# A decoder of four layers on one core: six layer normalisations moved to the head of the stages that follow them

## The reference

```python
def _layernorm(x, axis=-1, eps=1e-05):
    m = jnp.mean(x, axis=axis, keepdims=True)
    v = jnp.var(x, axis=axis, keepdims=True)
    return (x - m) / jnp.sqrt(v + eps)

x = x + attn(_layernorm(x), ...)          # L0 capped, L1 token mixing, L2 and L3 grouped-query
x = x + cross(_layernorm(x), ctx, ...)    # L3: the WKV recurrence with keys _layernorm(x), values ctx
x = x + ffn(_layernorm(x), ...)           # L0 MLP, L1 experts, L2 16 experts (4 chosen) + a shared one, L3 ternary
```

## Time and profile before

| | before |
|---|---|
| median of 3 runs | 1465.18 us (1462.57 to 1465.30) |
| the profiled execution's own time | 1461.6 us |
| its span, first to last instruction | 1459.9 us |
| mean granted TensorE clock | 0.893 of full speed |
| TensorE matmuls busy | 1221.0 us, 84% |
| TensorE weight loads busy | 755.3 us, 52% |
| VectorE busy | 794.9 us, 54% |
| ScalarE busy | 510.2 us, 35% |
| GpSimd busy | 319.6 us, 22% |
| mean DMA rate | 33 GB/s |

### The profile page before, as it was taken

One profiled execution on the slowest core, in us unless ns is written; L12 is line 12 of the kernel. 1 busy time (PEld: TensorE's weight loads), 2 busy tenths in 40 slices (PEclk: granted clock), 3 DMA queues, 4 the chain that ended last, 5 costly groups with the idle time before them and its releaser, 6 DMA issues. The chain is left out here.

```text
span 1459.9 us, 22518 instructions
## 1 busy us (share of the span) xinstructions
PE 1221.0 (84%) x8843; PEld 755.3 (52%) x8850; DVE 794.9 (54%) x2082; ACT 510.2 (35%) x934; POOL 319.6 (22%) x351
## 2 busy tenths in 40 slices
PE   3768679797958799779995997999999978985597
PEld 1335464465734554456663554555555545653354
DVE  2886757207577444657865665343111135767944
ACT  1018325313515433445444455111111114445443
POOL 0215402200002200135540221232222213440000
PEclk9878879898969599879996997999999987897799
DMA  9000000000040020000000000123233200000000
GB/s 367 1 0 2 1 1 2 0 0 1 0 188 1 8 109 0 1 1 3 3 2 0 2 2 1 49 62 101 80 97 90 87 15 1 2 2 0 1 1 29
DMA packets 13160, 47.95 MB, mean 33 GB/s; under 512 B 1640, under 2 KB 4712, under 8 KB 12288
## 3 DMA queue, kind: packets, MB, share of 16 engines
q1 hardware_dynamic: 13056, 46.53, 9.4%
HBM read 45.37 MB, written 1.15 MB: 32 GB/s over the span
## 5 line engine op out<-in xcount | busy, mean ns | idle before, releaser
L744 ACT ACTIVATE PT<-PS 128x384 f32<-128x384 f32 (+1 forms) x320 | 153.2, 531 | 214.0 <-PE PS L583 156.4
L1786 PE MATMUL PS<-HT,WA 128*128 128x512 f32 x448 | 201.4, 593 | 1.4 <-DVE MO L1854 1.4
L1854 DVE TENSOR_TENSOR MO<-PS,AO 128x512 f32<-128x512 f32 x56 | 38.7, 691 | 205.7 <-ACT AO L1844 205.6
L1786 PEld LDWEIGHTS PS<-HT,WA 128*128 128x128 f32 x448 | 84.7, 190 | 86.8 <-issue 82.9
L1844 ACT ACTIVATE AO<-PS 128x512 f32<-128x512 f32 x56 | 33.4, 597 | 252.1 <-PE PS L1786 252.1
L685 DVE CUSTOM_DVE_ANT_0 junk<-PS,TRI 128x128 bf16<-128x128 f32 (+1 forms) x384 | 113.0, 353 | 10.5 <-PE PS L564 7.0
L564 PE MATMUL PS<-KS,QM 32*128 32x128 f32 (+1 forms) x768 | 95.8, 383 | 19.5 <-PEq L897 8.7
L1794 PE MATMUL PS<-WA,HO 128*128 128x256 f32 x448 | 105.5, 378 | 0.0
L1794 PEld LDWEIGHTS PS<-WA,HO 128*128 128x128 f32 x448 | 84.5, 189 | 34.7 <-issue 24.9
L1908 POOL TENSOR_TENSOR HO<-MO,GR 128x512 f32<-128x512 f32 x44 | 57.9, 1316 | 168.6 <-PE PS L1794 168.6
L564 PEld LDWEIGHTS PS<-KS,QM 32*128 32x128 f32 x768 | 72.3, 206 | 42.9 <-issue 20.1
(11 more groups left out here) (314 smaller groups left out, 2390.4 us busy)
## 6 DMA issues: line engine op xcount, KB each, us to landing
WA<-w2f_in SPq DMA_DIRECT2D x28, 384.0 KB, 4.5
WA<-wl_in SPq DMA_DIRECT2D x1, 5137.0 KB, 15.8
GR<-gate_rows SPq DMA_DIRECT2D x20, 256.0 KB, 3.9
GB<-gate_rows SPq DMA_DIRECT2D x8, 512.0 KB, 7.6
WA<-wa_in SPq DMA_DIRECT2D x2, 1792.0 KB, 11.6
WB<-wb_in SPq DMA_DIRECT2D x1, 3208.0 KB, 18.5
WA<-wa_in SPq DMA_DIRECT2D x1, 2560.0 KB, 17.5
GR<-gate_rows SPq DMA_DIRECT2D x4, 448.0 KB, 3.8
```

What stands on the lines that cost most here:

```text
L744: act.activation(PT[:, g % 3, st_slot(k), 0:W], PS[:, st_bank(g, k), 0:W], ACT.Exp, scale=scale).then_inc(S["at_exp"], 1)
L1786: last = pe.matmul(PS[:, 2 * c + half, :], chunk(i, half)[:, k * P:(k + 1) * P], HT[:, k, c * CH:(c + 1) * CH], start=k == 0, stop=k == KD ...
```

## The change

`layernorm` is taken apart into `norm_steps`, which allocates the small tiles and returns each engine's list of steps, and a thin `layernorm` that puts them in a block as before. Four normalisations keep their block (the first, those behind layer 0's attention and layer 2's attention, and the one ahead of layer 1's experts). Six others lose it: their steps are called at the head of the next stage, inside its block. A new semaphore `ht` counts the copies to `HT`, `part_third` the third parts; `columns(engine, g)` waits until pair g is in place, `tokens(engine, g)` until its `H` is.

- MLP: TensorE does turn 0, turn 1, up (0, 0), turn 2, turn 3, up (0, 1). GpSimd's bias addition waits for the last `H`.
- Projections of layers 2 and 3: turn 0, turn 1, unit 0, turn 2 and unit 1, turn 3 and unit 2, then on; unit 4 waits for the last pair. The chunk is now the outermost part of the units' order.
- Experts of layer 2: turn 0, turn 1, router tile 0, turn 2 and tile 1, turn 3 and tile 2, then on; tile 4 waits for the last pair.
- WKV scan: output products and turns ahead of TensorE's sums; VectorE's whole normalisation behind the five setup instructions and ahead of the first scan.
- Ternary MLP: all turns first; up (0, 0) waits for the parts of the first two pairs, up (0, 1) for the rest. VectorE's and ScalarE's instructions of the split are interleaved with those of the normalisation.
- ScalarE and VectorE do the whole normalisation ahead of their own work of the stage, in all six.

```diff
-    def layernorm(src, dst, dstT=None, first=False, rows=None, pre=None, copies=None, parts=None):
+    def norm_steps(st, src, dst, dstT=None, first=False, rows=None, pre=None, copies=None, parts=None, tbank=None):
...
+        def columns(eng, g):
+            if parts is None:
+                eng.wait_ge(S["ht"], d["ht"] + g + 1)
+            else:
+                eng.wait_ge(S["part_third"], g + 1)
+
+        def tokens(eng, g):
+            eng.wait_ge(S["normed"], d["normed"] + 2 * g + 2)
...
+        def vector(dve):
+            for g in range(G + 4):
+                if g < G:
+                    measure(dve, g)
+                if 1 <= g <= G:
+                    apply(dve, g - 1)
+                if parts is not None and 3 <= g < G + 3:
+                    rest_of(dve, g - 3)
+                if parts is not None and g >= 4:
+                    third(dve, g - 4)
...
+        def scalar(act):
+            for g in range(G + 4):
+                if g < G:
+                    root(act, g)
+                if copies is not None and 1 <= g <= G:
+                    copies(act, g - 1)
+                if dstT is not None and 2 <= g < G + 2:
+                    copy(act, g - 2)
+                if parts is not None and g >= 4:
+                    second(act, g - 4)
...
-        work = [(w[a], a == "q", j, c) for a in ("q", "k") for j in range(2) for c in range(NCH)]
+        work = [(w[a], a == "q", j, c) for c in range(NCH) for a in ("q", "k") for j in range(2)]
...
+            norm = norm_steps(st, X, H, to_HT, tbank=lambda g: 4 + g, **norm_of)
...
+                    norm["turn"](pe, 0)
+                    norm["turn"](pe, 1)
                     for n, (a, _, j, c) in enumerate(work):
+
+                        if n == 0:
+                            norm["columns"](pe, 1)
+                        if n in (1, 2):
+                            norm["turn"](pe, n + 1)
+                        if n == 4:
+                            norm["columns"](pe, 3)
...
                     def go_up(i, c):
+                        if i == 0:
+                            norm["turn"](pe, 2 * c)
+                            norm["turn"](pe, 2 * c + 1)
+                            norm["columns"](pe, 2 * c + 1)
...
+                    norm["tokens"](pool, TT // 2 - 1)
                     pool.tensor_tensor(X[:], X[:], row, ALU.add).then_inc(S["pool_mark"], 1)
...
+                    norm["turn"](pe, 0)
+                    norm["turn"](pe, 1)
                     for t in range(TT):
+                        if t in (0, 4):
+                            norm["columns"](pe, t // 2 + 1)
+                        if t in (1, 2):
+                            norm["turn"](pe, t + 1)
...
                 def _(act):
+                    norm["scalar"](act)
                     sums(act, scratch[:], 0, 9)
...
                     dve.wait_ge(S["dve_chain"], d["dve_chain"] + 5)
+                    norm["vector"](dve)
                     gaps(0)
...
-        layernorm(X, H, to_HT)
         experts2(*scale_work)
-        layernorm(X, H, to_HT, pre=add_sums())
         left = grouped_attention(3, {"q": wL("q3", KD), "k": wL("k3", KD),
-                                  "v": wL("v3", KD), "o": wL("o3", KD)}, 16, 0.25)
-        finish(*left, dstT=to_HT)
-        wkv_scan()
+                                  "v": wL("v3", KD), "o": wL("o3", KD)}, 16, 0.25, pre=add_sums())
+        wkv_scan(*left)
         parts = sb("parts", [P, 3, KD, B * T], BF16)
-        layernorm(X, H, to_HT, parts=parts)
         ternary_mlp(exact, SC, parts)
```

More of the change, by code:

```diff
@@ L256, in _ @@
                 def _(dve):
[L257 to L268, removed]
@@ L278, in _ @@
[L278 to L288, removed]
-                            if g:
-                                dve.wait_ge(S["part_second"], g)
-                                dve.tensor_tensor(split(2, g - 1), rest(g - 1), split(1, g - 1), ALU.subtract)
+                    norm["vector"](dve)
@@ L293, in _ @@
                 @block.scalar
                 def _(act):
-                    def root(g):
-                        if first and g == 0:
-                            act.wait_ge(S["const_in"], 16)
-                        act.wait_ge(S["moments"], d["moments"] + 2 * g + 2)
-                        act.activation(std[:, 2 * g:2 * g + 2], mom[:, 2 * g:2 * g + 2, 1], ACT.Sqrt,
-                                       bias=cst("eps")).then_inc(S["std"], 1)
-                    def copy(g):
-                        act.wait_ge(S["turned"], d["turned"] + g + 1)
-                        src_ps = PS[:, tbank(g), :].rearrange("p (k n) -> p k n", k=KD)
-                        if parts is None:
-                            act.activation(dstT(slice(0, KD), g), src_ps, ACT.Copy)
-                        else:
-                            act.activation(split(0, g), src_ps, ACT.Copy).then_inc(S["part_first"], 1)
@@ L310, in second @@
-                    def second(g):
-                        act.wait_ge(S["part_rest"], g + 1)
-                        act.activation(split(1, g), rest(g), ACT.Copy).then_inc(S["part_second"], 1)
-                    for g in range(NG + 2):
-                        if g < NG:
-                            root(g)
-                        if copies is not None and 1 <= g <= NG:
-                            copies(act, g - 1)
-                        if g >= 2 and dstT is not None:
-                            copy(g - 2)
-                        if g >= 3 and parts is not None:
-                            second(g - 3)
@@ L323, in _ @@
-                    if parts is not None:
-                        second(NG - 1)
+                    norm["scalar"](act)
                 if dstT is not None or rows is not None:
@@ L328, in _ @@
                     def _(pe):
[L329 to L353 removed]
+                        norm["tensor"](pe)
     def add_product(dst):
@@ L1138, in turn_context_and_weights, with mlp @@
         done["turned"] += CTX + 8
-    def mlp(n, up, down, bias):
-        d = dict(done)
+    def mlp(n, up, down, bias, **norm_of):
         tag = str(nc.next_id())
@@ L1913, in experts2, with wkv_scan @@
                 done[name] += k
-    def wkv_scan():
-        d = dict(done)
+    def wkv_scan(left, pre, rows):
         tag = str(nc.next_id())
@@ L1926, in wkv_scan @@
             nw, nu = (tmp(x, [P, KD]) for x in ("nw", "nu"))
+            norm = norm_steps(st, X, H, to_HT, pre=pre, rows=rows)
+            d = dict(done)
+            done["dve_chain"] += 5
             K = HT[:].rearrange("p k (b t) -> p k b t", t=T)
@@ L2118, in ternary_mlp @@
             MP = tmp("MP3", [P, 3, NCH, CH], BF16)
+            norm = norm_steps(st, X, H, to_HT, parts=parts, tbank=lambda g: 4 + g)
+            d = dict(done)
             with nc.Block() as block:
```

160 lines of the change are left out of this document (108 added, 52 removed).

## The result

| | before | after |
|---|---|---|
| median, of 8 runs each | 1461.91 us (1459.66 to 1465.30) | 1454.12 us (1449.35 to 1458.85) |
| ratio of the times, 95% interval | | 0.9945 [0.993, 0.996] |
| profiled execution, own time | 1461.6 us | 1458.85 us |
| its span | 1459.9 us | 1457.1 us |
| its mean granted clock | 0.893 | 0.891 |

The change is faster by 7.8 us at the median, against 8.3 forecast from the trace; 1456.9 was forecast, in a range of 1452.6 to 1462.6. The profiled execution was the slowest of its eight, and its span is only 2.8 us shorter than that of before. So the comparison has to be made stage by stage.

The account below looks back on a forecast made before the run. TensorE, busy 84% of the span, was taken as the bound, idling at normalisations. Terms 0.7 + 2.1 + 0.4 + 2.0 + 1.9 + 1.2 = 8.3 us off the 1465.18 median gave 1456.9 us, range 1452.6 to 1462.6.

Parts of the forecast that it names:

- MLP: Layer 0's MLP: TensorE starts 2.84 us sooner, the first GELU waits for its table load; gain 0.7 us, 0 to 1.35.
- the low level lasts as long from the start as before: MLP of layer 0: transposes then run at the high clock level in 1.1 us and copy 4 ends at 273.8 us.
- rival A: All stages: the clock level rises at the same moments as before, so the gain is only 2.65 us, 1462.5 us; 13%.
- Projections of layer 2: Matmuls start 2.85 us sooner, with 4.4 us at the low level; gain 2.1 us, 0.3 to 2.5.
- Projections of layer 3: Matmuls start 2.96 us sooner, same steps as in layer 2; gain 2.0 us, 0.35 to 2.5.
- Experts: Router and experts of layer 2: wide matmuls start 0.9 us sooner, half survives; gain 0.4 us, 0 to 0.9.
- The reason given for the router's matmuls: Experts of layer 2: weight loads fill all 6.87 us of the narrow matmuls, which take the same at either level.
- Scan: WKV scan: no half starts early, only the block's edge goes; gain 1.9 us, between 1.0 and 2.0.
- Ternary MLP: First half ready 1.96 us sooner through the interleaved split; gain 1.2 us, 1.0 to 1.96.
- Rival B: All six sites: second-half copies or transposes hold up the first, only block edges go; 1.5 us, 1463.7 us; 6%.
- Rival C: MLP, projections, ternary MLP: broken work keeps TensorE at 1.2 GHz, 3.45 us more each; 5.5 slower, 1470.7 us; 5%.
- Rival D: Table load now on the path: a drain beside it takes 1.4 us off the gain, 1458.3 us; 4%.

Follow-up runs that it names:

- e10: The changed kernel itself, with no further edit, measured once more: 1453.15 us, 0.9914 of the kernel before.
- e2: The changed kernel with all four MLP turns ahead of its first product, which still waits for the first half only: 1450.57 us, 0.9915 of the kernel before.
- e1: The changed kernel with all turns first and first products waiting for the last pair, blocks still merged: 1457.94 us, 0.9976 of the kernel before.
- e3: The changed kernel with the MLP's GELU table loaded ahead of copies 3 and 4 by a one-column activation: 1455.14 us, 0.9944 of the kernel before.
- e5: The changed kernel with only the two projection stages' normalisations merged, the other sites in their own block again: 1456.49 us, 0.9954 of the kernel before.
- e6: The changed kernel with only the scan's and ternary MLP's normalisations merged: 1458.26 us, 0.997 of the kernel before.
- e7: The changed kernel with the MLP's and ternary MLP's normalisations in their own blocks, the split still interleaved: 1455.74 us, 0.9956 of the kernel before.
- e12: The kernel of e11 with more unread matmuls, enough to fill the pauses at the heads of both projections: 1445.01 us, 0.9865 of the kernel before.
- e11: The changed kernel with unread matmuls in TensorE's waits at the heads of the MLP and both projections: 1447.05 us, 0.9879 of the kernel before.
- e4: The kernel before with only the projections' unit order changed, chunk outermost: 1462.35 us, 1.0 of the kernel before.
- e8: The changed kernel with the first scan ahead of the last two H and exponentials ahead of copies 3 and 4: 1453.07 us, 0.993 of the kernel before.

## Why the prediction held, point by point

- *The sum and the cause.* The early halves, the missing edges and the scan give what was forecast in kind: 9.6 us by stage, 7.8 at the median, for 8.3. That the median came within 0.5 us is luck in part. The MLP came out 1.0 us worse than forecast and the other five together 2.3 better, some 2 us went in stretches that the forecast had left out, and the same pair of kernels measured again (e10) gave 12.6 us by the ratio.
- *MLP, the step that failed.* Forecast a gain of 0.7, bounds 0 to 1.35; measured a loss of 0.33, outside them. The step was "the low level lasts as long from the start as before". It rose at the old moment, so the first product and both turns behind it ran at 1.2 GHz for all the time won: 6.1 us of low level instead of 3.3. That is rival A, true at this site; in the experts the forecast had assumed it. With all turns first and the product directly behind them (e2) the level rises 3.4 us sooner and the MLP wins 67.26 - 64.94 = 2.3 us; with all turns first but a pause before the product (e1) it does not rise sooner. Why a pause of 0.69 us goes with the old moment is open. The table load behind copy 4, which the forecast had priced by the path, is 0.28 of it (e3).
- *Projections of layer 2.* 2.1 forecast, 2.81 measured. The rise moved with the matmuls. The forecast had read the end of a row, 608.60, as the rise, which came 0.5 us later: the low part was 5.7 us before, not 5.2, and 5.5 after, not 4.4, two errors that nearly cancel. The last spreading of keys ended at 636.40, 34.8 us after the stage's start, before at 631.18 - 594.43 = 36.8: 2.0 sooner, as forecast. It ends 4.0 us after TensorE's last product, as before, so ScalarE's chain stayed covered; TensorE's attention starts 2.0 sooner. The other 0.8 came inside the attention, which the forecast had not looked at.
- *Projections of layer 3.* 2.0 forecast, 2.28 measured, by the same steps; the low part, 5.3 us, was again longer than assumed. The low parts of both projections and of the MLP are above the 5 us that the forecast had named as the most.
- *Experts.* 0.4 forecast, 0.84 measured. As assumed, the level rose at the old moment and half of the earlier start was lost: the shared gate's wide matmuls began 1.3 us sooner (897.60 - 883.04 against 894.55 - 878.72) and the product behind them 0.7. The transposes between the router's matmuls took back 1.5 us, not 1.7 to 2.0. The reason given for the router's matmuls, that they take the same at either level, is not borne out: their weight loads took 0.33 us each at 0.50, and the first MLP's loads of the same shape ranged from 0.34 to 0.19. It cost nothing here, for the router ran low before and after. VectorE's wait for the sum over partitions shrank from 4.94 to 2.95 us and did not go: the late start of ScalarE's sums stayed hidden.
- *Scan.* 1.9 forecast, 2.29 measured. Against e5, where the block is kept behind the same stage, it is 59.81 - 57.90 = 1.91; behind layer 3's projections with the length of before it is 60.19 - 58.93 = 1.26 (e6). The rest hangs on the stage ahead; that it is VectorE's wait for the output product, at whatever clock that finds, was not tested.
- *Ternary MLP.* 1.2 forecast, 1.71 measured: the first product came 2.15 us sooner (10.6 after the stage's start, before 12.76) and the rise by about 1.5 of that. e7 and e1 (86.67 and 86.21 us, both interleaved, both without the early half) show that it is the early half, not the interleaving.
- *Rival B* (only edges) is out: e1 loses three quarters of the stages' gain by waiting alone. *Rival C* (slower by a longer low level) is out: the low stretches measured 5.5, 5.3 and 4.3 us in projections and ternary MLP, against 5.7, 5.1 and 3.6 before. The MLP's grew most, from 3.3 to 6.1 us, and none reached 7. *Rival D* (a drain beside the load) is out. The Trainium skill, "ScalarE: Activation LUTs", section "What ACT_TABLE_LOAD costs", puts about 1380 ns of drain beside a load. Here copy 4 ended at 278.86, the load ran from 278.88 to 280.16 and the GELU began at 280.17.
- *Against the median.* The forecast set the sum against 1465.18, of three runs; with eight the kernel before stands at 1461.91. So 1456.9 lay 2.8 above what was measured.

## What to carry to other kernels

Let a stage's first half start as soon as its own input is there, and put the previous stage's tail in the same block: the early halves gave three quarters of 9.6 us here, the missing edges with the rest one quarter. But look where the first matmuls land in TensorE's clock. Where the level rises at the old moment, half of the time won goes again (experts) or all of it (MLP), and the same MLP with its turns and its first product in one unbroken run was 2.65 us shorter. If TensorE must wait at a stage's head, matmuls without a use that fill the wait were worth another 7 us (e12 against e10, by their ratios 0.9865 and 0.9914), against 12.6 for the change itself by e10's ratio.

## What was not expected of the hardware

- The level falls in the pauses of a normalisation: in layer 3 with pauses of 2.62 and 1.55 us (e11, in the second of them), while with pauses of 0.46, 0.25 and 0.93 us at the same place it stayed (e12). The first product of a stage then takes 1.98 us instead of 3.78.
- The same code at the same place took 163.10, 166.31 and 163.29 us (first attention) and 146.01, 148.16 and 148.09 (mixing and cross-attention of layer 1) in three profiles, at clocks of 0.85 against 0.83 and of 0.87 against 0.84. In e4, whose code is that of before up to there, the second took 147.73. Over all fourteen profiles the first attention, the same code in all, took 161.5 to 166.3 us. The eight runs of the changed kernel spread over 9.5 us with clocks of 0.891 to 0.903: the clock's moments in unchanged stages outweigh any single term of the sum.
- A stage that ends sooner can cost the next one: of 1.7 us won in the scan 0.84 was lost again in the ternary MLP (e8), and behind the faster projections of layer 2 in e11 the cross-attention took 1.4 more (104.74 to 106.13) and the experts 1.4 less (314.05 to 312.66). Why the rise comes later there is open; no run set the start of a stage against the clock alone.
